# Feed-forward norm and output projection by halves, first products on the rounded half, and a new order of calls, in a two-layer kernel on one Trainium2 core

## The reference

```python
# layer 0: adaptive norm, causal attention (16 heads, norm on q and k), adaptive norm, feed-forward
h = layernorm(x) * (1 + ca) + sa
x = x + ga * attention(h)
h = layernorm(x) * (1 + cb) + sb
f = silu((h @ w1.T) * s1) * ((h @ w2.T) * s2)      # 256 -> 1024, weights are -1, 0 or 1
f = gelu((f @ h1.T) * sh1)                          # 1024 -> 1024
f = gelu((f @ h2.T) * sh2)                          # 1024 -> 1024
x = x + gb * ((f @ w3.T) * s3)                      # 1024 -> 256
# layer 1: adaptive norm, selective scan (512 channels, 16 states), adaptive norm, quantised projection
h = layernorm(x) * (1 + ca) + sa
x = x + ga * selective_scan(h)
h = layernorm(x) * (1 + cb) + sb
x = x + gb * (quantise(h) @ quantise(W).T + bias)
```

## Time and profile before

| | us |
|---|---|
| median of 3 runs (lowest to highest) | 4162.34 (4157.99 to 4164.06) |
| the profiled execution's own time | 4167.61 |
| span of that execution, first to last instruction | 4165.8 |
| one steady pass, from its first `project` to that of the next | 235.1 |
| of it: attention and the work beside it | 125.7 |
| of it: norm of the feed-forward, `up`, `mid(0)` | 37.5 |
| of it: the other `mid` products, to the next `project` | 71.9 |

### The profile page before, as it was taken

How to read it: one execution, slowest core, us unless ns; L and a number is a source line. 1 busy time by engine, 2 the same in 40 slices (tenths; PEclk the granted TensorE clock), 3 DMA queues, 4 the chain that set the end, 5 groups by cost and what they waited for, 6 DMA issues and landing times. The chain is left out here.

```text
span 4165.8 us, 50421 instructions
## 1 busy us (share of the span) xinstructions
PE 3523.9 (85%) x16621; PEld 2034.0 (49%) x16621; DVE 3318.2 (80%) x3646; ACT 2583.4 (62%) x3703; POOL 2716.0 (65%) x1960
## 2 busy tenths in 40 slices
PE   5687888989899998989898898989999898989513
PEld 3263645546373645546373554636364554636201
DVE  4514878989798888979797887979898897979694
ACT  2345566767667676766666676767667676666431
POOL 0132866768595876768595776759586776768563
PEclk9799999999999999999999999999999999999756
DMA  4630201102030301103030211203030211203000
GB/s 164 258 105 15 97 21 62 62 26 97 6 117 1 97 26 61 62 21 102 6 102 17 82 41 46 77 8 115 1 107 16 76 46 41 82 6 102 0 5 5
DMA packets 69435, 247.81 MB, mean 59 GB/s; under 512 B 9472, under 2 KB 10112, under 8 KB 68736
## 3 DMA queue, kind: packets, MB, share of 16 engines
q1 hardware_dynamic: 66816, 235.35, 16.8%
q10 hardware_dynamic: 2304, 8.39, 0.5%
HBM read 212.25 MB, written 31.46 MB: 59 GB/s over the span
## 5 line engine op out<-in xcount | busy, mean ns | idle before, releaser
L671 POOL TENSOR_TENSOR kept<-kept,hb 128x512 f32<-128x512 f32 x640 | 811.0, 1300 | 71.1 <-DVE hb L1925 70.9
L1916 DVE TENSOR_TENSOR_SCAN hb<-ps,hb 128x512 f32<-128x512 f32 x640 | 745.0, 1205 | 17.5 <-ACT ps L1362 12.7
L929 PE MATMUL ps<-hid_bhi,wring 128*128 128x512 f32 x1536 | 628.0, 409 | 70.9 <-issue 53.6
L929 PE MATMUL ps<-hid_blo,wring 128*128 128x512 f32 x1536 | 619.8, 404 | 0.0
L1362 ACT ACTIVATE ps<-kept,a_neg 128x512 f32<-128x512 f32 x640 | 423.0, 690 | 174.4 <-DVE hb L1916 174.4
L929 PE MATMUL ps<-hid_ahi,wring 128*128 128x512 f32 x1280 | 516.7, 404 | 8.0 <-POOL hid_alo L686 8.0
L639 POOL TENSOR_TENSOR kept<-kept,hb 128x1024 f32<-128x1024 f32 x128 | 300.2, 2360 | 336.3 <-DVE hb L1860 297.7
L929 PE MATMUL ps<-hid_alo,wring 128*128 128x512 f32 x1280 | 505.0, 395 | 0.0
L632 POOL TENSOR_SCALAR_AFFINE_SELECT room<-room 128x512 f32<-128x512 f32 x256 | 217.7, 862 | 427.2 <-ACT room L1569 427.2
L1988 DVE TENSOR_REDUCE room<-ps 128x4 f32<-128x2048 f32 (+3 forms) x256 | 375.2, 1486 | 123.6 <-PE ps L1105 111.3
L1925 DVE TENSOR_TENSOR hb<-hb,ps 128x512 f32<-128x512 f32 x640 | 404.0, 673 | 0.1
(11 more groups left out here) (198 smaller groups left out, 7359.2 us busy)
## 6 DMA issues: line engine op xcount, KB each, us to landing
wring<-w_hi SPq DMA_DIRECT2D x352, 512.0 KB, 3.3
...
```

The costliest lines, as they stand in the source:

```text
L671: pool.tensor_tensor(acc[:, m, :], acc[:, m, :], hb[:, s % 8, :], ALU.add).then_inc(acc_done, 1)
L929: mm = pe.matmul(bank(bk), wring[:, r % 3, at + k * P:at + (k + 1) * P], src[i][:, k, :], start=(k == 0 and i == 0), stop=(k == K - 1 and ...
L1916: dve.tensor_tensor_scan(hb[:, s % 8, :], bank(2 + m % 2), hb[:, s % 8, :], 0.0, ALU.mult, ALU.add).then_inc(scanned, 1)
```

## The change

- The norm of the feed-forward gets semaphores of its own (`f_mean` to `f_norm`), and `ffn_mean`, `ffn_var`, `ffn_centre`, `ffn_square` and `ffn_scale` take one half of the features each. `ffn_affine` falls into `ffn_round(c)` and `ffn_full(c)`.
- `att_proj(quad, m)` makes one half of the output; the halves stand in the list one by one.
- `up(0)` and `up(1)` fall into `up_high` (the four products with the rounded half, which wait only for that) and `up_low` (those with the rest).
- The rest of the weights is no longer stored. The flag is asked for once ahead of the feed-forward: the list of products stands twice in the program, with the unrounded weights (`wraw`) and with the rounded ones, and one of the two is run. The first tiles of rounded weights are loaded earlier in the first pass.
- The lists of calls of all four engines stand in another order, from the start to the end of a pass.

```diff
+            def wait_tile(r, exact):
...
+            def product(bk, r, at, src, K, exact, fresh=None):
                 for k in range(K):
-                    if k == K - 1:
-                        with pe.If(has_rest > 0):
...
+            def up_high(n, exact):
                 if ffn:
-                    if n >= 2:
-                        pe.wait_ge(gated_up, since(gated_up, n - 1))
-                    elif n == 0:
-                        pe.wait_ge(h_rounded, since(h_rounded, DC))
-                        pe.wait_ge(h_split, since(h_split, DC))
+                    pe.wait_ge(h_rounded, since(h_rounded, DC))
+                    wait_tile(0, exact)
...
+            def up_low(n, exact):
+                if ffn:
+                    pe.wait_ge(h_split, since(h_split, DC))
+                    up_product(n, 1, exact).then_inc(up_done, 1)
...
-            def ffn_mean():
+            def ffn_mean(c):
                 if ffn:
-                    pe.wait_ge(att_added, since(att_added, DC))
-                    pe_mean(pe, xa, k_ffn, 4)
+                    pe.wait_ge(att_added, since(att_added, c + 1 if att else DC))
+                    mm = pe.matmul(bank(4), mean_mat[:, :], xa[:, c, :], start=(c == 0), stop=(c == DC - 1))
...
+            def ffn_centre(c):
                 if ffn:
-                    dve_centre(dve, xa, k_ffn, 4)
+                    dve.wait_ge(f_mean, since(f_mean, 1))
+                    dve.wait_ge(ln_out, k_ffn.outs)
+                    dve.tensor_tensor(ln_x[:, c, :], xa[:, c, :], bank(4), ALU.subtract).then_inc(f_cent, 1)
...
+            if ffn:
+                with pe.If(has_rest > 0):
+                    feed_forward(False)
+                with pe.Else():
+                    feed_forward(True)
```

615 lines of the change are left out of this document (324 added, 291 removed).

## The result

| | before | after |
|---|---|---|
| median (lowest to highest), us | 4163.2 (4157.99 to 4175.95) | 4256.2 (4250.55 to 4287.36) |
| ratio, 95% interval | | 1.0234 (1.0188 to 1.0281) |
| span of the profiled execution, us | 4165.8 | 4285.6 |
| a steady pass, first `project` to the next `project` | 232.2 to 235.7 | 237.8 to 245.6 |
| its attention part, to the last `att_proj` | 122.0 to 126.3 | 131.1 to 137.6 |

The rows of the whole pass and of its last stretch leave out the pass in which the loop turns; there the stretch behind `att_proj` takes 119.0 us before and 120.8 after.

A forecast was written before the change was run, and what follows sets the result against it. PE, POOL and DVE were taken as full in the last stretch, latencies as binding attention and norm. Terms -0.7 - 1.1 - 2.0 + 0.1 = -3.7 us a pass, times 16 = -59, gave 4103 us, range 4062 to 4160.

The forecast's parts named there:

- Mean by halves: Feed-forward norm, end of `att_proj` to end of mean: 2.1 instead of 2.83 us, -0.7 a pass (0 to -1.0).
- Centre, square, variance: Feed-forward norm, mean to variance's end: pipelined by halves, 3.2 to 3.3 instead of 4.39 us, -1.1 a pass.
- First products and gates: Feed-forward's start: products need only rounded copies, PE starts 2.2 us earlier, last gate -2.6 us, `mid(0)` -2.5.
- V: The moment the variance in the feed-forward's norm ends, from which the forecast counts later times in us.
- Body: Last gate to next pass: DVE decides, with 2.7 us more calls behind `gate_up(7)`; -2.0 a pass kept (0 to -2.5).
- The flag: Feed-forward's start on PE: one jump over 374 products, about 3.5 us, covered by the wait for the rounded half.
- Sum of these: Norm, feed-forward and body together, without attention: -0.7 - 1.1 - 2.0 us a pass.
- Attention: Attention part, new order of all four lists: losses and gains nearly cancel, +0.1 us a pass (-2.5 to +3).
- The edges: First pass's loads and vanished stores: 0, within 10 us a run; last two passes: 0, within 5.
- Rival C: Attention: two more table loads and `att_proj` products unhidden, 4.3 to 6.2 us a pass lost; 4181 us, chance 0.14.
- rival A: Attention gains as well, no engine being full there: -2.1 us a pass more, 4070 us, chance 0.20.

The follow-up runs named there:

- 4184: Changed kernel with the old order of calls up to about 65 us into a pass (first two quads), seam moved by two calls: 4183.7 us, ratio 1.0041.
- the four at the end together: Changed kernel with `invert_sums(2)`, `weigh(2)`, `att_proj(2, 1)` and `fin_back(0)` moved at the end of the attention part: 4246.2 us, ratio 1.0181.
- both edits: Changed kernel with the old order of the first two quads and the four calls moved at the end of the attention part: 4161.7 us, ratio 0.9990.

## Why the prediction was wrong, step by step

- **Mean by halves**: right. 2.27 us from `att_proj` to the mean; 2.1 was said, 2.83 before.
- **Centre, square, variance**: right, a little small. 3.49 from the mean to the variance; 3.2 to 3.3 was said, 4.39 before.
- **First products and gates**: right, within 0.4. First product at V + 4.91 (4.9 was said), first gate at V + 10.4 (10.8), the second directly behind, the last ends at V + 24.3 (24.65). The clock's fall behind the first product is gone in all 14 steady passes. In 8 of them it comes some 7 us later, which gives 1.6 back (the rest is 108.3 us there, 106.7 where it stays out); the prediction had no term for it. The window, in the second pass shown above:

```profile
3634.40:3637.80 3.40, 3.39 (x9) 2.76 (x10) 2.85 (x3) 1.32 (x4) 3.09 (x3) 0.58 0.21 86
```

- **Body**: half right. From the last gate to the next pass 76.65 us after, 74.92 before: 1.7 more, and 0.6 was said. DVE's idle time ahead of the first `normalise` fell from 3.50 to 1.52, as said. No run took apart what the other 1.1 us are.
- **The flag**: right, and shown by the run without it.
- **Sum of these**: -3.8 a pass was said. The trace has -2.7 in the best passes, -1.1 in the others, and -1.7 in the mean.
- **Attention**: this step failed. It said +0.1 with bounds of -2.5 and +3; the trace has +9.0 in the mean of 14 passes (125.4 to 134.4), and +6.7 with `pick_mod`'s waits taken out; that this order is the whole of the loss is shown by the kernel with the old one. The step listed ACT's two table loads against ACT's idle 3.15 us, found them covered, and stopped there. On ACT they are: in the changed kernel the third exponential starts 5.13 us behind the second, before 5.51. But the silu between them frees a bank for PE, and that PE would wait was not asked: cover on the engine that works says nothing on the engine that reads. The run that moves this silu alone, in the old order, shows it, with 86 us; in the changed kernel, whose PE list has other waits at that place, taking it back gains nothing. The walk also ended behind the second quad, and 4256 - 4184 is only part of the loss. "Those `values` wait for a `weigh` anyhow" was true and no comfort, for `weigh(2)` itself had moved back, behind calls on two engines.
- **`pick_mod`** was not in the prediction at all. The order showed the move; what POOL does at the new place was not asked.
- **The edges**: bounds of 10 us, and the first pass alone is 13 us longer in its attention part, the second 10.

Rival C had the side, the place and nearly the point from which it decides (a loss over 3.8 us), but its mechanism, the two loads in the chain of exponentials, is not what was found, and its 4181 us were 75 too few. Of rival A the premise was right (no engine is full in the attention part), and it works both ways: a part that hangs on latencies is as easily made longer. Three of the prediction's smaller sums don't come out, without weight for the result: A's -2.1 a pass stands beside a bound of -2.5, 4070 less 10 is 4060 and not 4062, and nine products at 0.233 us leave 1.3 of the 3.4 us and not 1.6.

What stays open: the loss in the changed kernel is not the sum of few calls. Single calls taken back in it, and the four at the end together, give 10 us at most; three calls put singly into the old lists cost 45 to 86 (of these only the silu was also taken back), and only whole stretches of the four lists bring the time back. Of the 31 us that stay with both edits, the trace lays the larger part to the late `gate_out`, and the rest is not explained. What each call of the first two quads has in the 72 us is open too.
